# A two-layer graph kernel: pair 0's gates in front of the third pair's transposes, gate biases negated in the front, first dense product in the order of its halves, shifts by GpSimd

## The reference, cut to what matters

```python
h = jnp.maximum(_layernorm(x), 0.0)
# layer 0 (adj_a = adj_b = adj)
attn_a = sigmoid(concat([adj @ h, h]) @ Wa.T + ba)       # one gate per node
attn_b = sigmoid(concat([adj @ h, h]) @ Wb.T + bb)
hs = h @ W_sa
scores = (hs @ a_left)[:, None] + (hs @ a_right)[None, :]
e = where(adj != 0, exp(-leaky_relu(scores, 0.01)), 0.0)
x_a = (e / (sum(e, axis=1, keepdims=True) + 1e-5)) @ hs
x_b = adj @ (h @ W_gcnb) + b_gcnb
x = x + sigmoid(attn_a * x_a + attn_b * x_b)
# layer 1
h = jnp.maximum(_layernorm(x), 0.0)
pooled = (dinv * (adj + I) * dinv) @ h + h               # dinv = rsqrt(degree)
x = x + relu(pooled @ W + b)
```

## Time and profile before

| | |
|---|---|
| median of 3 runs | 611.3 us |
| profiled execution | 611.8 us |
| its span (first to last instruction) | 610.0 us |
| TensorE busy | 593.4 us, 97% of the span |
| VectorE busy | 425.2 us, 70% |
| ScalarE busy | 362.4 us, 59% |
| GpSimd busy | 255.5 us, 42% |

### The profile page before, as it was taken

The page is one execution under the profiler, slowest core; times in us unless marked ns, Lnnn a source line. Parts: engine busy times, 40 slices in busy tenths (PEclk is TensorE's granted clock), DMA queues, the critical chain, the costliest instruction groups (busy, mean ns, idle before and its releaser), DMA issues.

```text
span 610.0 us, 13250 instructions
## 1 busy us (share of the span) xinstructions
PE 593.4 (97%) x5265; PEld 508.4 (83%) x5265; DVE 425.2 (70%) x811; ACT 362.4 (59%) x878; POOL 255.5 (42%) x361
## 2 busy tenths in 40 slices
PE   7889998999999999999999999999999999999996
PEld 5446687888888888888888888888888888888886
DVE  6897885999998999899989989988753121111111
ACT  3687667797887979797979788979642000000000
POOL 3664313554453435343525276313132374435433
PEclk8999999899999999999999999999999999999999
DMA  8908399957566565647474745010400486546401
GB/s 198 225 3 113 111 134 249 203 83 182 94 150 121 123 134 110 146 98 162 81 177 67 190 52 79 2 19 1 130 2 18 113 318 215 174 157 193 144 20 35
DMA packets 55801, 73.60 MB, mean 121 GB/s; under 512 B 20027, under 2 KB 47933, under 8 KB 54331
## 3 DMA queue, kind: packets, MB, share of 16 engines
q0 software_dynamic: 28544, 22.15, 26.5%
q1 hardware_dynamic: 24754, 46.42, 23.5%
q10 hardware_dynamic: 2441, 4.20, 2.2%
HBM read 69.31 MB, written 22.16 MB: 150 GB/s over the span
## 4 chain that ended last, share of the span: by engine, by line
PE 82%; DVE 5%; DMA 4%; issue 4%; POOL 4%; ACT 2%; ACTq 0%; POOLq 0%; DVEq 0%
PE accE L786 11%; PE accE L788 11%; PE accE L787 11%; PE accA L764 10%; PE accA L765 10%; PE accA L831 7%; PE accA L830 7%; PE accE L830 4%; PE accE L831 4%; DMA stage<-in_adj_dram 3%; POOL stage L369 1%; DVE bst L933 1%; PE pw L803 1%; PE accA L847 1%; PE pw L805 1%
## 5 line engine op out<-in xcount | busy, mean ns | idle before, releaser
L786 PE MATMUL accE<-HI,Z 128*128 128x257 f16 x676 | 185.2, 274 | 2.4 <-DVE wm L1078 2.1
L788 PE MATMUL accE<-HI,E 128*128 128x257 f16 x676 | 184.8, 273 | 0.0
L787 PE MATMUL accE<-LO,Z 128*128 128x256 f16 x676 | 184.7, 273 | 0.0
L549 ACT ACTIVATE Z<-LO,sr 128x256 f32<-128x256 f32 x338 | 151.4, 497 | 35.6 <-PE accE L788 35.6
L764 PE MATMUL accA<-HI,adjT 128*128 128x260 f16 x676 | 154.0, 273 | 0.0
L765 PE MATMUL accA<-LO,adjT 128*128 128x258 f16 x676 | 154.0, 273 | 0.0
L558 ACT ACTIVATE Z<-Z,sr 128x256 f32<-128x256 f32 x338 | 150.1, 496 | 0.2
L1034 DVE TENSOR_TENSOR Z<-adjT,Z 128x512 f32<-128x512 bf16 x169 | 127.0, 751 | 17.1 <-ACT Z L558 16.1
L1040 DVE TENSOR_TENSOR E<-Z 128x512 bf16<-128x512 f32 x169 | 129.0, 763 | 5.8
L369 POOL DMA_DIRECT2D stage<-in_adj_dram x96 | 59.3, 649 | 93.0 <-DVE adjT L1026 88.6
L831 PE MATMUL accA<-LO,adjT 128*128 128x256 f16 x416 | 91.6, 273 | 0.0
(11 more groups left out here) (127 smaller groups left out, 721.0 us busy)
## 6 DMA issues: line engine op xcount, KB each, us to landing
adjT_store<-adjT SPq DMA_DIRECT2D x11, 1664.0 KB, 6.3
stage<-in_adj_dram POOLq DMA_DIRECT2D x48, 192.0 KB, 5.0
stage<-in_adj_dram POOLq DMA_DIRECT2D x36, 224.0 KB, 5.2
adjT<-adjT_store SPq DMA_DIRECT2D x7, 896.0 KB, 6.0
adjT<-adjT_store SPq DMA_DIRECT2D x7, 768.0 KB, 6.0
stage<-adjT_store SPq DMA_DIRECT2D x4, 896.0 KB, 6.4
stage<-adjT_store SPq DMA_DIRECT2D x4, 768.0 KB, 5.8
out_dram<-late ACTq DMA_DIRECT2D x11, 256.0 KB
```

Source lines behind the costliest of these rows:

```text
L549: ins = act.activation(Z[:, n % RING, v], slw[:, m], ACT.Relu, bias=sr99[:, t:t + 1], scale=1.0 - SLOPE)
L786: pe.matmul(dst[:, 0:D + 1], zhi, HI[:, t, 0:D + 1], start=(t == 0), stop=False)
L787: pe.matmul(dst[:, 0:D], zhi, LO[:, t, 0:D], start=False, stop=False)
L788: ins = pe.matmul(dst[:, 0:D + 1], zlo, HI[:, t, 0:D + 1], start=False, stop=(t == TILES - 1))
```

## The change

Five edits.

1. VectorE: `gate_args(0)` and `gates(0)` come before `turn_adj(2, 0)`; `turn_adj(2, 1)` moves from unit 4 of pair 1 (behind `row_sums(0)`) to unit 6.
2. GpSimd: nbias is made in the front, behind `load_adj(0, 1)`.
3. The shifts nmr are made by GpSimd in `inv_stds` (nmean = -mean, then nmean * rstd), no longer by VectorE.
4. TensorE's first dense product (`dense_first`) takes the first halves of both weights first, then hTl, then the second halves, with turn(1) in between; turn(2) and project(0) stand between the halves of dense(1), and turn(3), project(1) behind it; ScalarE puts turned(1) between the two copies of pair 0.
5. VectorE's order in the front: W1's maximum and diagonal, the scales of W1 and the score weights, and the diagonal of pair 0's scores come later, the statistics are one pair further back in the loop.

```diff
 # GpSimd, inv_stds(n)
                 pool.tensor_tensor(ve[:, a:b], mv[:, a:b, :, 1], epss[:, 0:b - a], ALU.add).then_inc(vplus, 1)
+                pool.tensor_scalar(nmean[:, a:b], mv[:, a:b, :, 0], -1.0, None, ALU.mult).then_inc(nmean_ok, 1)
                 pool.wait_ge(vplus, n + 1)
                 pool.tensor_tensor(rstd[:, a:b], ve[:, a:b], halfs[:, 0:b - a], ALU.pow).then_inc(rstd_ok, 1)
+                pool.wait_ge(nmean_ok, n + 1)
+                pool.wait_ge(rstd_ok, n + 1)
+                pool.tensor_tensor(nmr[:, a:b], nmean[:, a:b], rstd[:, a:b], ALU.mult).then_inc(nmr_ok, 1)
...
             load_adj(0, 1)
+            pool.wait_ge(bias_in, 32)
+            pool.tensor_scalar(nbias[:], bias2[:], -1.0, None, ALU.mult).then_inc(nbias_ok, 1)
...
             load_adj(3, 0)
-            pool.wait_ge(bias_in, 32)
-            pool.tensor_scalar(nbias[:], bias2[:], -1.0, None, ALU.mult).then_inc(nbias_ok, 1)
             with_bias(0)
 # ScalarE
             def turned(i):
                 act.wait_ge(hT_ps, i + 1)
+                if 2 <= i <= 3:
+                    act.wait_ge(proj, i - 1)
...
                 if s == 0:
-                    first_halves(0)
+                    first_half(0, 0)
                 if s + 1 < PAIRS:
                     turned(s + 1)
+                if s == 0:
+                    first_half(0, 1)
                 if s + 2 < PAIRS:
                     norm(s + 2)
...
-                if s == 1:
+                if s == 3:
                     left_first()
 # TensorE
             def dense(i):
...
                 for e in range(2):
+                    if i == 1 and e == 1:
+                        turn(2)
+                        project(0)
+                    pe.wait_ge(lo_ok, 2 * i - 1 + e)
...
+            def dense_first():
+                rows = [slice(e * P, (e + 1) * P) for e in range(2)]
+                pe.wait_ge(hTh_ok, 1)
+                for k in range(2):
+                    pe.wait_ge(whi_ok, k + 1)
+                    for e in range(2):
+                        for h in range(HALVES):
+                            pe.matmul(bank(dn, e)[:, k * D:(k + 1) * D], hTh[:, 0, h, rows[e]],
+                                      wh[:, h, k * D:(k + 1) * D], start=(k == 0 and h == 0), stop=False)
+                pe.wait_ge(hTl_ok, 1)
+                for e in range(2):
+                    for h in range(HALVES):
+                        pe.matmul(bank(dn, e), hTl[:, 0, h, rows[e]], wh[:, h], start=False, stop=False)
+                turn(1)
+                pe.wait_ge(wlo_ok, 2)
+                for e in range(2):
+                    for h in range(HALVES):
+                        ins = pe.matmul(bank(dn, e), hTh[:, 0, h, rows[e]], wl[:, h], start=False,
+                                        stop=(h == HALVES - 1))
+                    ins.then_inc(dn_ps, 1)
...
             for s in range(PAIRS):
-                dense(s)
+                dense(s) if s else dense_first()
                 if s == 0:
-                    turn(1)
-                    project(0)
+                    keep_busy(8)
+                if s == 1:
+                    turn(3)
+                    project(1)
+                if s == 2:
                     spread_weights(2, 4, 2)
-                    keep_busy(4)
-                if s == 1:
+                    project(2)
+                if s == 3:
                     widen_first()
-                if s + 2 < PAIRS:
+                if 2 <= s and s + 2 < PAIRS:
                     turn(s + 2)
...
-                if s + 1 < PAIRS:
+                if s >= 2 and s + 1 < PAIRS:
                     project(s + 1)
 # VectorE
...
-            turn_adj(2, 0)
             gate_args(0)
             gates(0)
+            turn_adj(2, 0)
...
                     if u == 4:
                         row_sums(m - 1)
-                        if m == 1:
-                            turn_adj(2, 1)
+                    if m == 1 and u == 6:
+                        turn_adj(2, 1)
```

More of the change, by code:

```diff
@@ L82, in gnn_kernel @@
         nmr = sb("nmr", [P, PAIRS, 2])
+        nmean = sb("nmean", [P, PAIRS, 2])
         unused = sb("unused", [P, 1])
@@ L176, in gnn_kernel @@
         vplus = sem("vplus")
+        nmean_ok = sem("nmean_ok")
         rstd_ok = sem("rstd_ok")
@@ L524, in first_weights, with first_half @@
                 act.activation(dst, src, ACT.Copy, scale=winv[:, (0, 1, 3)[k]:(0, 1, 3)[k] + 1]).then_inc(whi_ok, 1)
-            def first_halves(i):
+            def first_half(i, e):
                 src = dn[:].rearrange("p (e k d) -> p e k d", e=2, k=2)
-                for e in range(2):
-                    act.wait_ge(dn_ps, 2 * i + e + 1)
-                    dst = bass.AP(HI[:].tensor, (2 * i + e) * HIW, [[TILES * HIW, P], [G0, 2], [1, D]])
-                    act.activation(dst, src[:, e], ACT.Copy).then_inc(hi_ok, 1)
+                act.wait_ge(dn_ps, 2 * i + e + 1)
+                dst = bass.AP(HI[:].tensor, (2 * i + e) * HIW, [[TILES * HIW, P], [G0, 2], [1, D]])
+                act.activation(dst, src[:, e], ACT.Copy).then_inc(hi_ok, 1)
             def left_first():
@@ L620, in _ @@
                 if 0 < s < PAIRS:
-                    first_halves(s)
-                if s == 1:
+                    first_half(s, 0)
+                    first_half(s, 1)
+                if s == 3:
                     left_first()
@@ L938, in row_stats @@
                 ins.then_inc(stats, 1)
-            def minus_mean(n):
-                a, b = BATCHES[n]
-                dve.wait_ge(rstd_ok, n + 1)
-                dve.scalar_tensor_tensor(out=nmr[:, a:b], in0=mv[:, a:b, :, 0], scalar=-1.0, in1=rstd[:, a:b],
-                                         op0=ALU.mult, op1=ALU.mult).then_inc(nmr_ok, 1)
             def score_weights():
@@ L962, in on_diagonal @@
             def on_diagonal(k0, k1):
+                dve.wait_ge(consts, 5)
                 dve.wait_ge(wabs_ok, k1)
@@ L1003, in diagonal_first, with second_half @@
                 ins.then_inc(diag_ok, 1)
-            def second_halves(i):
-                for e in range(2):
-                    dve.wait_ge(hi_ok, 2 * i + e + 1)
-                    first = bass.AP(HI[:].tensor, (2 * i + e) * HIW, [[TILES * HIW, P], [G0, 2], [1, D]])
-                    dve.tensor_tensor(LO[:, 2 * i + e, 0:2 * D].rearrange("p (k d) -> p k d", k=2),
-                                      bank(dn, e).rearrange("p (k d) -> p k d", k=2), first,
-                                      ALU.subtract).then_inc(lo_ok, 1)
+            def second_half(i, e):
+                dve.wait_ge(hi_ok, 2 * i + e + 1)
+                first = bass.AP(HI[:].tensor, (2 * i + e) * HIW, [[TILES * HIW, P], [G0, 2], [1, D]])
+                dve.tensor_tensor(LO[:, 2 * i + e, 0:2 * D].rearrange("p (k d) -> p k d", k=2),
+                                  bank(dn, e).rearrange("p (k d) -> p k d", k=2), first,
+                                  ALU.subtract).then_inc(lo_ok, 1)
             def turn_adj(m, c):
@@ L1117, in _ @@
             largest(0, 1)
-            minus_mean(0)
             largest(1, 2)
             on_diagonal(0, 2)
-            minus_mean(1)
             gate_weights()
@@ L1129, in _ @@
             row_stats(2)
+            second_half(0, 0)
+            turned_second(1)
+            second_half(0, 1)
+            row_stats(3)
+            take_scores(0)
+            turned_second(2)
+            second_half(1, 0)
+            second_half(1, 1)
             dve.wait_ge(w1_in, 16)
@@ L1132, in _ @@
             on_diagonal(2, 4)
-            second_halves(0)
-            minus_mean(2)
-            take_scores(0)
-            turned_second(1)
-            row_stats(3)
-            diagonal_first()
-            scales(2, 4, 2)
+            take_scores(1)
             row_stats(4)
-            minus_mean(3)
+            row_stats(5)
             turns = {5: (0, 0), 6: (0, 1), 10: (1, 0), 11: (1, 1)}
-            for s in range(1, PAIRS + 6):
-                if s < PAIRS:
+            for s in range(2, PAIRS + 6):
+                if 2 < s < PAIRS:
                     take_scores(s)
@@ L1147, in _ @@
                     turned_second(s + 1)
+                if s < PAIRS:
+                    second_half(s, 0)
+                    second_half(s, 1)
                 if s == 2:
-                    minus_mean(5)
-                if s < PAIRS:
-                    second_halves(s)
-                if s in (1, 3, 5):
-                    minus_mean({1: 4, 3: 6, 5: 7}[s])
-                for j in (2 * s + 3, 2 * s + 4):
+                    take_scores(2)
+                    scales(2, 4, 2)
+                    diagonal_first()
+                for j in (2 * s + 2, 2 * s + 3):
                     if j < PAIRS:
```

4 lines of the change are left out of this document (removed).

## The result

The changed kernel takes 615.71 us (median of 6 runs, 614.67 to 616.85) against 610.46 for the kernel before (6 runs, 610.36 to 613.11): ratio 1.0077, 95% interval 1.0056 to 1.0098. It is 5.3 us slower by the medians and 4.7 by the ratio. Forecast were 612.8, a range of 608.5 to 616.5, and slower with a chance of 0.30: the range held the time, the direction went to the smaller chance, and the time was 2.9 us short. The forecast stood on a median of 611.3 for the kernel before, which is 610.46 here; as a difference to before, +1.5 was forecast, which is 3.2 to 3.8 short.

The account below looks back on a forecast made before the run. VectorE's queue was taken to bound the front, TensorE the rest from the marker on, less a seam loss. Front +5.4 and seam -3.9 gave +1.5 on 611.8, 613.3, or 612.8 against the median; range 608.5 to 616.5.

Parts of the forecast that it names:

- Seam: Passage from pair 0 to pair 1: earlier gates remove TensorE's 2.22 us idle and 1.71 of half clock, gain 3.93.
- GpSimd's timetable: At the seam: with_bias(0) ends at 99.5, 1.8 us before row_sums(0) asks; contention with VectorE might add 0.6.
- Front: From 15 us to turned_second(8): VectorE's queue sets it, new idle makes that marker 5.4 us late, range 4.5 to 7.
- three LO waits: VectorE waits before the second halves of pairs 1, 2 and 3's dense products: 2.7, 1.7 and 1.9 us.
- (B): Rival, faster: front bound by TensorE's own order, VectorE's new idle not passed on; about 606.5 us, chance 0.17.
- I take 0: Front, clock after the second new TensorE wait (1.6 us): dense(4) read 1.0 later, 0 to +1.7, taken as 0.
- (C): Rival, slower: clock falls at new TensorE waits while ScalarE awaits dense products; 3.4 for two stretches, 615 us, chance 0.23.
- second assumption: Front, after the first new TensorE wait (2.2 us): dense(2) has until norm(4) ends at 29.4, hiding the half clock.
- At nothing: Front items priced at zero, among them gate_columns(0), waiting for the scales until 32, needed only after 45.
- (D): Rival at the seam: late load delays with_bias(0), TensorE idles again, only 1 of 3.9 gained; 615.7 us, chance 0.10.

Follow-up runs that it names:

- e2_front: The changed kernel with the edits between pair 0 and pair 1 (gates order, nbias) undone, front edits alone: 617.47 us.
- e9_queue: e5_refill with GpSimd's inverse deviations of batch 5 (pairs 5 and 6) ahead of gate_columns(0): 610.81 us.
- e5_refill: The changed kernel with statistics of pairs 4 and 5 and W1's maximum and diagonal before LO(1), later statistics one pair further ahead: 613.47 us.
- e12_best: e10_clock with 10 instead of 20 filler products ahead of dense_first, and nbias on GpSimd behind batch 5: 610.51 us.
- e3_stats: The changed kernel with the statistics of pairs 4 and 5 moved into VectorE's wait before LO(1): 613.19 us.
- e10_clock: e9_queue with 20 filler products on TensorE in front of turn(3), in its wait before dense(2): 609.82 us.
- e4_filler: The changed kernel with 16 filler products behind widen_first(), in TensorE's 1.86 us wait before dense(4): 615.53 us.
- e11_seam3: The kernel before with edits 1 and 2 alone (pair 0's gates before the third pair's transposes, nbias in the front), timed again: ratio 0.9986.

## Why the prediction was right or wrong

**Seam: size and mechanism right for the profiled pair** (3.97 for 3.93). The exponent came 0.38 behind zg, the wait and the half clock were gone. Wrong was to take as the typical cost: the 1.09 us for a DMA in the earlier trace rows was the sign that a good quarter of it was a landing time, and the half clock another 1.7 that the next profile didn't have. In medians the seam brought about 1 at the front of before, and 1.6 behind the late front of the changed kernel (e2_front).

**GpSimd's timetable: margin too large.** I gave with_bias(0) 1.8 us of slack before row_sums(0). It ended at 109.2, 1.8 us before row_sums(0) at 110.99, but only because VectorE was late as well: the 256-column pair took 2.18 (1.85 before), the 512-column add 1.74 (1.27), VectorE's split beside it 1.65 (0.69). The Trainium skill (GPSIMD Engine Reference, Key points) says that GpSimd shares its SBUF interfaces with VectorE and contends with VectorE instructions that have two SBUF inputs. The trace agrees, on both sides of it: 0.8 us longer on GpSimd where I had 0.6, and about 1.5 on VectorE (the split 0.96 and three products of 0.85 to 0.90 for 0.69), which I had at nothing. TensorE's margin shrank to about 0.6 us (wm ends near 112.5, wanted at 113.17).

**Front: mechanism right, size short by 2.4.** The three LO waits came as worked out, each within about 0.3 us, so (B) falls: VectorE's idle was passed on whole. The term that failed is the clock, "I take 0" of "0 to +1.7": behind TensorE's wait of 1.86 us the clock fell while dense(4) was wanted, LO(4) waited 1.42, and (C) was right for that place. The second assumption there, that dense(2) hides its half clock behind norm(4), held in the changed kernel, where dense(2) was done 0.8 before HI(2) began: in e9_queue, with the statistics early, the same half clock cost 1.5 on LO(2). Whether the clock falls at such a wait differs from profile to profile, so this term is a price with a chance, and 0 was a choice and not a measurement. The remaining 1.0 of the 2.4 is 0.5 at LO(1) and LO(3) (2.95 and 2.21 for 2.7 and 1.9) and small gaps that no single row holds. With the head's 1.07 below, these 2.4 make up, within 0.1, the 3.4 by which the profiled span (+4.9) passed the forecast (+1.5).

**"At nothing": gate_columns(0).** I asked who needs its result (nobody before 45) and not who is queued behind it. In the changed kernel that costs little, since the statistics of pair 6 are themselves late (34.8; the chain begins at 35.13). It becomes 2.5 us of the front as soon as they are not (e5_refill against e9_queue). The 20 filler products ahead of dense_first may be another such place: in before they end about when the second halves come (12.5 us), and with 10 of them dense_first starts at 11.94. But e12_best moved nbias as well, and no run parts the two.

**Head: +1.07** that I had at nothing, and rightly for the code: it lies within what one and the same kernel shows (14.23 to 16.66). (D) did not occur.

Undone step by step, the front went from 42.10 to 39.12 (statistics), 38.72 (whole wait filled), 36.27 (GpSimd's queue), 35.50 (clock) and 34.60 (filler and nbias), against 34.30 before: 7.5 of the 7.8 us are found. The sum is firmer than its parts. Each step is one profile, the same kernel's front lies between 34.46 and 35.21 in three, and the half clock came and went between them without an edit aimed at it (dense(2) in e3_stats, LO(4) in e5_refill). In medians the way from the changed kernel to e10_clock is 6.0 us by the distances to before.

## What to carry to other kernels

When a change moves an instruction later, list what is queued behind each instruction that waits for it, on every engine; "its result is needed late" is no cover. Before you price a wait, look whether the chain in front of it holds a DMA wait: that part moves from run to run, and a single profile tells its size for that execution alone. Cut the spans of all variants at two or three fixed instructions: here the rest repeated within 0.2 us over nine of the ten profiles with the seam edits, and showed at once in which part a difference lay. And before you credit an edit with a clock that stayed full, look for a kernel without the edit in which it stayed full too.

## What the runs showed of the hardware

- The granted clock of TensorE fell to its half level (1.2 of 2.4 GHz) behind waits of 2.58 and 1.86 (changed kernel), 2.06 (before), 2.13 (e2_front), 1.87 (e3_stats), 2.58 (e5_refill) and 3.15 us (e9_queue), but stayed full behind 2.79 (second profile of before), 2.23 (e2_front), 2.19 (e3_stats), 2.10 and 2.33 (e4_filler) and 1.86 us (e5_refill): the length of the wait alone doesn't tell.
- With filler in such a wait the clock stayed full in the profiles of the three kernels that had it (16 products in e4_filler, 20 in e10_clock and e12_best). For e10_clock and e12_best more executions than the profiled one speak for the filler, by their mean clock: 0.998 or more in seven and five of twelve, against 0.997 at most in e9_queue. For e4_filler none do.
- The same 20 filler products took 2.63 us in e9_queue and 3.85 us in e10_clock, at a granted clock that reads 1.00 in both.
- Profiled executions of before lay at 611.8 both times, above its medians of 610.5 to 611.2; those of e9_queue, e10_clock and e11_seam3 lay within 0.3 of theirs, that of e12_best 1.1 below.
- Where GpSimd's and VectorE's instructions ran side by side at the seam, both took longer: a 256-column pair on GpSimd 2.18 us instead of 1.85, a 512-column split on VectorE 1.65 instead of 0.69.
